# Expert weights loaded into the freed feed-forward blocks, and expert tiles placed in the slots of the loop's last five steps

## The reference

```python
x = x + attention0(layernorm(x))                    # 16 heads
x = x + feed_forward(layernorm(x))                  # silu(gate) * up, 256 -> 1024 -> 256
x = x + attention1(layernorm(x))                    # 16 query heads on 4 key heads
h = layernorm(x)
scores = einsum('btd,ed->bte', h, Wg)               # 8 experts
topk_s, topk_i = top_k(scores, 2)
w = einsum('btk,btke->bte', softmax(topk_s), onehot(topk_i))
for e in range(8):
    y = y + w[..., e:e+1] * ((silu(h @ W1[e].T) * (h @ W2[e].T)) @ W3[e].T)   # hidden 176
x = x + y
```

## Time and profile before

| | |
|---|---|
| three runs | 1286.82, 1291.46, 1289.36 us, median 1289.36 |
| the profiled execution | 1285.61 us, span 1283.9 us |
| busy | PE 86%, DVE 57%, ACT 44%, POOL 35% of the span |
| PE clock granted, mean | 0.91 of full speed |
| tiles | from 992.8 to 1244.4 us |
| gathers of group 1, adds, output | from 1244.4 us to the end |

### The profile page before, as it was taken

One profiled execution on the slowest core, in us unless ns is written; L12 is line 12 of the kernel. 1 busy time (PEld: TensorE's weight loads), 2 busy tenths in 40 slices (PEclk: granted clock), 3 DMA queues, 4 the chain that ended last, 5 costly groups with the idle time before them and its releaser, 6 DMA issues.

```text
span 1283.9 us, 27492 instructions
## 1 busy us (share of the span) xinstructions
PE 1105.1 (86%) x8482; PEld 908.3 (71%) x8482; DVE 737.3 (57%) x1985; ACT 569.1 (44%) x1252; POOL 447.6 (35%) x608
## 2 busy tenths in 40 slices
PE   3989999999989799999999999999774978997870
PEld 2766666667656698888888888888653857775750
DVE  3567676676753555566666666664547645444543
ACT  2145455554544344555555555553332534553330
POOL 4234444444432111224333343444355130014516
PEclk9599999999998999999999999998755978998885
DMA  6344444344440461001111111111222332334545
GB/s 217 110 119 139 117 135 116 118 140 117 132 115 27 140 210 34 22 25 42 42 40 40 40 44 40 40 42 62 79 94 70 104 116 79 99 108 139 153 130 166
DMA packets 98580, 122.17 MB, mean 95 GB/s; under 512 B 16054, under 2 KB 85884, under 8 KB 98492
## 3 DMA queue, kind: packets, MB, share of 16 engines
q1 hardware_dynamic: 91580, 102.17, 25.8%
q0 software_dynamic: 6912, 18.88, 4.6%
HBM read 64.37 MB, written 56.10 MB: 94 GB/s over the span
## 4 chain that ended last, share of the span: by engine, by line
PE 60%; DVE 14%; ACT 8%; issue 7%; POOL 4%; another core or an unknown queue 3%; DMA 1%; DVEq 1%; SPq 0%; POOLq 0%; ACTq 0%
PE bank L963 4%; PE bank L1579 3%; PE bank L876 3%; PE bank L1581 3%; PE bank L1580 3%; DVE a_negm L1291 3%; PE bank L878 2%; PE bank L877 2%; PE bank L583 2%; PE bank L600 2%; PE bank L608 2%; PE bank L598 2%; PE bank L623 2%; PE bank L599 2%
## 5 line engine op out<-in xcount | busy, mean ns | idle before, releaser
L1172 ACT ACTIVATE a_prob<-bank 128x512 f32<-128x512 f32 x192 | 114.2, 598 | 134.6 <-PE bank L963 134.1
L1579 PE MATMUL bank<-b_xF_hi,wff_hi 128*128 128x256 f32 x512 | 154.0, 301 | 2.2 <-DVE b_xF_lo L1939 1.4
L1291 DVE TENSOR_REDUCE a_negm<-bank 128x2 f32<-128x512 f32 (+1 forms) x192 | 129.7, 683 | 37.7 <-PE bank L930 37.7
L1580 PE MATMUL bank<-b_xF_lo,wff_hi 128*128 128x256 f32 x512 | 145.7, 285 | 0.1
L1581 PE MATMUL bank<-b_xF_hi,wff_lo 128*128 128x256 f32 x512 | 145.6, 284 | 0.0
L1396 POOL TENSOR_SCALAR_AFFINE_SELECT a_prob<-a_prob 128x1024 f32<-128x1024 f32 x64 | 70.0, 1094 | 169.2 <-ACT a_prob L1172 169.2
L820 POOL DMA_INDIRECT m_ring<-y_sorted,b_k_rows x64 | 61.7, 964 | 167.8 <-DMA y_sorted<-m_y 128.5
L930 PE MATMUL bank<-a_K,a_Q 48*128 48x256 f32 (+1 forms) x512 | 111.4, 319 | 0.0
L963 PE MATMUL bank<-a_Q,a_K 50*128 50x256 f32 (+1 forms) x512 | 106.8, 310 | 0.4 <-ACT a_prob L1172 0.4
L1947 DVE TENSOR_TENSOR b_hf<-bank,b_sg 128x256 f32<-128x256 f32 x128 | 53.9, 421 | 89.4 <-ACT b_sg L1802 85.4
L1579 PEld LDWEIGHTS bank<-b_xF_hi,wff_hi 128*128 128x128 f32 x512 | 97.9, 191 | 7.7 <-DVE b_xF_lo L1939 1.6
(11 more groups left out here) (269 smaller groups left out, 3214.7 us busy)
## 6 DMA issues: line engine op xcount, KB each, us to landing
scr<-a_split SPq DMA_DIRECT2D x64, 256.0 KB, 2.4
a_Q<-scr SPq DMA_DIRECT2D x192, 64.0 KB, 2.2
a_K<-scr SPq DMA_DIRECT2D x192, 64.0 KB, 2.3
m_xs<-x_sorted SPq DMA_DIRECT2D x78, 128.0 KB
y_sorted<-m_y SPq DMA_DIRECT2D x78, 128.0 KB
x_sorted<-b_r_zeros SPq DMA_DIRECT2D x1, 6016.0 KB, 19.9
parts<-b_split SPq DMA_DIRECT2D x16, 256.0 KB
out<-x_res SPq DMA_DIRECT2D x16, 256.0 KB
```

Of the source, the lines that this page charges most:

```text
L1172: nc.scalar.activation(o, src, ACT.Exp, scale=float(HD) ** -0.5).then_inc(S.exps, 1)
L1291: nc.vector.tensor_reduce(R.negm[:, p, j, c0:c0 + n], ps[bank][:, :].rearrange("p (h k) -> p h k", h=n), axis=AX.X, op=ALU.max, negate=Tru ...
L1579: pe.matmul(o, wh, xh, start=(c == 0), stop=False)
L1580: pe.matmul(o, wh, xl, start=False, stop=False)
```

## The change

1. **Weights.** The feed-forward's weights are laid out in eight blocks of 768 columns, block m holding all that slot m uses. Ten blocks of 768 make up the experts' weights. Their raw form is loaded straight into the place of `wff_lo` (`wraw` shares its memory), copied to `wff_hi` by ACT and replaced by the difference. Blocks 8 and 9, which the feed-forward never used, are loaded behind SP's step 14; blocks 0 to 5 in step 15, each once `down` of the last sequence has used it; 6 and 7 in step 16, between the store of sequence 14's queries and keys and the loads of their stacks. ACT's copies stand in (15,0), (15,1), (15,5), (15,6), (15,7) and (16,0) to (16,4); POOL makes the first six differences, all at the end of its step 15, DVE the last four in (16,1) to (16,4).
2. **Tiles in slots.** The loop ends with step 20 in place of 18. From (16,5) on each slot begins with one expert tile on PE, ACT and DVE, tiles 0 to 34; tile 35 and those behind it follow the loop. SP starts loading tiles behind step 16, and its step 17 comes behind the load of tile 9.
3. **Banks.** The tiles have one bank for transposes in and for `hT` together (0), one for the product (1) and one for `down` (2) while i < 21; from there the product alternates between 1 and 3, and `hT` has 5. So `up(k)` waits for the product of k-1 in the narrow part, `hT(k)` for the transposed tile k+2, and `xT(k)` for the subtraction of `hT(k-3)`.
4. **What `rest` did** for sequences 14 and 15 goes back into the steps 19 and 20.
5. **Tables.** `v_table` is cut into three parts: group 0's in (15,4), (15,6) and (18,4), group 1's in (20,4), (20,5) and (20,7).

```diff
-NMAIN = 12
+FF_BLOCK = 2 * NC * P + E
+NMAIN = WD_MAIN // FF_BLOCK
...
         wff_hi = sb("wff_hi", [P, WMAX], F32R)
+        with ExitStack() as raw_weights:
+            wraw = raw_weights.enter_context(nc.sbuf_tensor("wraw", [P, WMAX], F32))
         wff_lo = sb("wff_lo", [P, WMAX], F32R)
...
             def sp(eng):
                 for i in range(NTILES + 8):
+                    if i == 10:
+                        layer["sp_step"](eng, NSEQ + 1, 1)
...
+                        if i == 0:
+                            eng.wait_ge(layer["S"].up, NSEQ * INTER0 // P)
...
+            XT, DOWN = 0, 2
+
+            def up_bank(i):
+                return 1 if i < NARROW or i % 2 == 0 else 3
+
+            def hT_bank(i):
+                return XT if i < NARROW else 5
...
+                def xT(k):
+                    eng.wait_ge(S.loaded[k % 4], 16 * (k // 4 + 1))
+                    if k >= 1:
+                        eng.wait_ge(S.xT_lo, k)
+                    if k >= 3 and k - 3 < NARROW:
+                        eng.wait_ge(S.hT_lo, k - 2)
...
+                def up(k):
+                    eng.wait_ge(S.xT_lo, k + 1)
+                    if k >= 1:
+                        eng.wait_ge(S.h, k if k <= NARROW else k - 1)
...
+                def hT(k):
+                    eng.wait_ge(S.h, k + 1)
+                    if k < NARROW:
+                        eng.wait_ge(S.xT_lo, min(k + 3, NTILES))
+                    elif k >= 1:
+                        eng.wait_ge(S.hT_lo, k)
...
+                if i == 0:
+                    eng.wait_ge(layer["S"].h, NSEQ * INTER0 // P)
+                    eng.wait_ge(layer["S"].ffres, NSEQ)
+                    eng.wait_ge(S.table, 1)
+                    offsets(0)
+                    xT(0)
+                    xT(1)
+                    eng.wait_ge(wf.lo1, NMAIN)
+                    eng.wait_ge(wf.tail, 3 * NTAIL)
...
-            first, end, last = 6, 14, NSEQ + 2
+            def tile_of(t, m):
+
+                return NM * (t - NSEQ) + m - 5
+
+            def with_tile(t, m):
+                return isinstance(t, int) and t >= NSEQ and tile_of(t, m) >= 0
...
                     elif m > 2 and live(t):
                         pe_down(pe, t, m - 2)
+                    if with_tile(t, m):
+                        X1["pe"](pe, tile_of(t, m))
...
+            def main_block(k):
+
+                b = (k + NM) % NMAIN
+                return [w[:, b * FF_BLOCK:(b + 1) * FF_BLOCK] for w in (wff_hi, wff_lo, wraw)]
...
+            HI_AT = {(15, 0): 0, (15, 1): 1, (15, 5): 2, (15, 6): 3, (15, 7): 4, (16, 0): 5, (16, 1): 6, (16, 2): 7,
+                     (16, 3): 8, (16, 4): 9}
+            LO_AT = {(16, 1): 6, (16, 2): 7, (16, 3): 8, (16, 4): 9}
...
+            TABLE_AT = {(15, 4): (0, 0), (15, 6): (0, 1), (18, 4): (0, 2), (20, 4): (1, 0), (20, 5): (1, 1), (20, 7): (1, 2)}
...
-                if isinstance(t, int) and NSEQ <= t < NSEQ + 3:
-                    for n in range(4):
-                        p_weights(pool, 4 * (t - NSEQ) + n)
+                if isinstance(t, int) and t == NSEQ - 1:
+                    for k in range(NMAIN - len(LO_AT)):
+                        p_weights(pool, k)
...
                     sp_out(sp, t - 2, p)
+                    if isinstance(t, int) and t == NSEQ:
+                        sp_weights(sp, 8)
+                        sp_weights(sp, 9)
                     sp_stacks(sp, t - 2, p)
...
+            def sp_weights(sp, k):
+
+                b = (k + NM) % NMAIN
+                if b < NM:
+                    sp.wait_ge(S.down, NM * (NSEQ - 1) + b + 1)
+                if k >= 4:
+                    sp.wait_ge(wf.hi1, k - 3)
+                sp.dma_start(main_block(k)[2], w_moe[:, b * FF_BLOCK:(b + 1) * FF_BLOCK])\
+                    .then_inc(wf.in1[k % 4], 16)
+
+            first, end, last = 6, 14, NSEQ + 4
```

More of the change, by code:

```diff
@@ L482, in uses, with v_table @@
                 return len(range(k, n, depth))
-            def v_table(dve, n, g):
+            LINKED = (7, 12, 7)
+            CLEARED = sum(LINKED[:2]) + 2
+            COUNT = {(g, part): g * sum(LINKED) + sum(LINKED[:part]) + 2 * ((g, part) >= (0, 2)) for g in range(2) for part in range(3)}
+            NARROW = 21
+            def v_table(dve, g, part):
                 grp = TOKENS[g]
                 steps, tiles = grp.cap // P, grp.tiles
-                o = [S.count, n]
+                o = [S.count, COUNT[g, part]]
                 def linked(instruction):
@@ L495, in v_table @@
                 one = slice(0, P)
[L496 to L524, removed]
@@ L531, in v_table @@
-                nc.vector.tensor_copy(table[:, 1, :], R.local[0:1, 0:tiles]).then_inc(S.table, 1)
-                items = 4 * (grp.seqs[1] - grp.seqs[0])
-                mine = cols(4 * grp.seqs[0], items)
-                big = R.big[:, 0:items * NEXP].rearrange("p (i e) -> p i e", e=NEXP)
-                jump = R.load
-                linked(nc.vector.tensor_tensor(R.until, R.until, R.each, ALU.subtract))
-                linked(nc.vector.scalar_tensor_tensor(out=R.until, in0=R.until, scalar=-float(P), in1=R.base[:, g, :],
-                                                      op0=ALU.mult, op1=ALU.add))
@@ new lines, in dve @@
+                if i == 0:
+                    for k in range(2):
+                        nc.vector.memset(R.h[:, k, :], 0.0).then_inc(S.count, 1)
+                    xT(0)
+                    xT(1)
+                if i < NTILES:
+                    h(i)
+                if 1 <= i <= NTILES:
+                    hT(i - 1)
+                if i + 2 < NTILES:
+                    xT(i + 2)
+                if i == TOKENS[1].tile:
+                    eng.wait_ge(route.S.weights, NSEQ)
+                if i >= TOKENS[1].tile + 6:
+                    for _ in range(2):
+                        if done[0] < end_item[0]:
+                            add(eng)
@@ L804, in pool, with sums @@
+            def sums(eng):
+                while done[0] < len(items):
+                    add(eng)
             def pool(eng):
[L805 to L808 removed]
                 first = 0
@@ L2218, in run @@
                 for t in range(end, last + 1):
+                    if engine == "sp" and t == NSEQ + 1:
+                        return
                     step(eng, t, t % 2)
-            return dict(S=S, run=run, v_f_ln=v_f_ln, p_f_ln=p_f_ln, pe_oT=pe_oT, pe_out=pe_out, act_oT=act_oT, v_oT=v_oT, v_res=v_res)
+                if engine != "pool":
+                    for i in range(tile_of(last, NM - 1) + 1, NTILES + 2):
+                        X1[engine](eng, i)
+            return dict(S=S, run=run, v_f_ln=v_f_ln, p_f_ln=p_f_ln, sp_step=sp_step)
         def first_ln(eng, engine, old, new):
```

453 lines of the change are left out of this document (198 added, 255 removed).

## The result

Four runs of the changed kernel gave 1268.40 to 1281.25 us, median 1273.96, beside four of the kernel before with a median of 1288.94: ratio 0.9871, 95% interval 0.9837 to 0.9904, so 15 us or 1.3% faster. The forecast of 1280 had the sign; against its 9 us the gain was 1.6 times as large.

A forecast was written before the change was run, and what follows sets the result against it. Bound: the drain's chain of waits, then PE's work. 940.1 + 21.4 + 125.2 + 13.5 = 1100.2 against 1107.9 at tile 35, 7.7 us less; between 1277.9 and 1281.6 it chose 1280 us, 8-in-10 range 1248 to 1302.

The forecast's parts named there:

- part 1: Step 15 and start of step 16: POOL's differences delay the table (+9.7 us, bounds 0 to 12), DVE's add 1.1.
- part 2: Slots (16,5) to (16,7): waits, three tiles partly at half clock, a Silu table load and attention work, 21.4 us.
- step 17: Eight slots with a tile each: 22.4 us of tiles, 9.8 of attention work, 3.2 of stalls, 35.4 together.
- step 18: Eight slots with a tile each: 22.4 us of tiles, 7.3 of attention work, 5.2 of stalls, 34.9 together.
- step 19: Eight slots with a tile each: 21.5 us of tiles, 3.6 of attention work, 1.6 of stalls, 26.7 together.
- step 20, burst and scatters: Step 20's tiles, attention work and stalls, 28.2 us, plus POOL's twelve DMAs, 10.5, and scatters in steps 17 and 18, 3.
- (15,4) at nothing: Seven table operations in slot (15,4), where PE is full: 0 to 1.5 us, taken as 0.
- part 4: POOL's DMA bursts: twelve in a row in step 20, 10.5 us; scatters of fours in steps 17 and 18, 3.
- the marker: Start of tile 35's first matmul, first tile behind the loop: 1107.9 us before, 1100.2 forecast, nothing changing behind it.
- B: PE's pace holds: no POOL hold on DVE, stalls covered, narrow slots free; 30 us less, 1250; chance 0.20.
- C: Half clock among the tiles of steps 17 to 20: 4.32 us a slot, 1300 at one whole step; chance 0.24.
- D: Nothing moves: late blocks or loads leave tiles standing in (16,5) and step 17; 1288 us; chance 0.12.

The follow-up runs named there:

- e9: Changed kernel with group 0's first two table parts in slots (15,0) and (15,2) instead of (15,4) and (15,6); ratio to before 0.9897.
- e2: Changed kernel with POOL's six weight differences waiting until the second part of group 0's table is written; ratio to before 0.9876.
- e12: Changed kernel with POOL's six weight differences on DVE in (16,0) and (16,4), table parts in (15,0) and (15,2); 1270.81 us, ratio 0.9853.
- e1: Changed kernel with group 0's first two table parts in slots (14,4) and (14,6) instead of (15,4) and (15,6); ratio to before 0.9868.
- e6: Changed kernel without tiles in the slots: all tiles behind step 20, with two product banks; 1279.82 us, ratio to before 1.0174.
- e8: Changed kernel with POOL's eight fill DMAs of group 1 each waiting for a tile's product; 1241.09 us, ratio to before 0.986.

## Why the prediction was right, and where it was off

The forecast was right in sign and in where the time goes, and low in size: it set tile 35 at -7.7 us; it came at -16.5 on the chip of the result, and 3.4 were lost again behind it. The steps of the sum (from (16,1) to (16,5) before took 12.3, after 13.4):

| step of the sum | forecast | first chip | second chip |
|---|---|---|---|
| part 1: delay of (16,1) | 10.8 | 12.4 | 12.1 |
| and up to (16,5) | 0 | 1.0 | |
| part 2: start of the tiles to tile 3 | 21.4 | 17.6 | 18.6 |
| step 17 | 35.4 | 36.9 | 35.5 |
| step 18 | 34.9 | 34.1 | 35.3 |
| step 19 | 26.7 | 27.6 | 26.7 |
| step 20, burst and scatters | 41.7 | 32.7 | 23.4 |
| behind tile 35 | 0 | +3.4 | +0.4 |

- **Part 1.** Right in place and nearly in size: the table part lasted 9.9 us where 9.7 was said. The mechanism under it was half wrong. I let one operation be held for all four splits, after the 6.51 of the earlier trace rows; each was held for one. Why one was held for four in before stays open. The Trainium skill (SBUF — State Buffer, section "SBUF: two separate sides") has it so: an exclusive lock kept for one instruction. The rows of this kernel and of e9 agree with that. What was wrong is my price for it, about 6 us for the part: turn by turn it cost 9.9, since four operations were held for 0.9 to 1.6 each, 5.6 in sum, on top of the 4.3 that the part takes without splits (e2). That this met my 9.7, worked out from another picture, is luck. Splits five and six went on to hold two more (at 924.60 for 1.82 us and at 929.48 for 1.79; the upper bound of 12 that I named). What I had wrong is that the cost belongs to the table: e9 and e12 show that it belongs to the splits, and most of it, 6.9 us by e9's rows, stays when the table is moved away.
- **(15,4) at nothing:** right. From (15,1) to the projection in (15,6) the changed kernel takes 20.0 us and before 19.7, on the second chip. For the second part the slot matters: e1 showed no slack in (14,6).
- **Part 2** was 3 to 4 us too dear: the clock was 0.80 in it (0.75 on the second chip), and I had reckoned a part of the products at half clock for longer.
- **Steps 17 to 19** were within 1.6 us in sum, but two errors may lie under that. A narrow slot costs 0.79 more where it is bare, not 0.14: I took DVE's subtraction to delay the transposes once, by what it was late, and overlooked what stands behind them on PE, the reading of the offsets ahead of the transpose of h. In steps 17 and 18 attention work stands between the two and covers a part, and my stalls for ranking and exponentials made up the rest. The total was right; the division between them wasn't measured.
- **Step 20 and part 4** are the term that failed. The burst, 10.5, was sized well for this chip: tile 34 to 36 lost 12.6 us there and 3.0 on the other, so 9.6. But the scatters (3) did not show in steps 17 and 18; where one group did, in step 19 on the first chip, tiles 21 to 27 took 18.4 instead of 17.5. And the rest of step 20 took 23.4, not 28.2: tiles 27 to 34 came every 2.7 us, so its attention work (1.7) and its ranking (0.8) cost nothing, and of the 4.5 for the table's pieces 3.0 showed, in (20,7) and behind, 2.0 of it ahead of the marker. That is 9 us of the difference.
- **Behind the marker** 3.4 came back on this chip. 1.5 of it is tile 35 to 36 at half clock after the stall, the rest was not traced.
- **Rivals.** B (1250) asked for POOL not to hold DVE and for narrow slots at no price; both fail. C's half clock did not come: 0.91, 0.95 and 1.00 in steps 17 to 19. e6 shows what it is like when it does, without tiles to fill the slots. D is refuted by tile 35.

## What to carry to other kernels

Filling the slots of a draining pipeline with independent work gave 34 us at tile 35 (e6 against the changed kernel), and a higher clock for the drain's own work; bringing the inputs early is only what makes it possible, and gave nothing alone. Give a small job to the engine and the slot whose wait it can fill, and look up which instruction that wait stands in front of: one place further it is on the path (e1, e12). A POOL subtraction on SBUF beside a chain of small DVE operations with two inputs in SBUF cost the chain up to 1.6 of its 1.8 us for each; here it was cheaper to do the POOL work on DVE (0.93 against 1.8 us) than to move the chain.

## What the hardware showed that I had not expected

- The same kernel took 1274 to 1278 us on one kind of chip and 1246 on another. The difference went with waits of ACT whose end the trace can't name, 40 us in sum on the one and none on the other. All 19 of them in the kernel after begin within 1.6 us of the start of one of POOL's indirect DMAs. That these cause them was not tested where they occur: e8 ran on the second chip. At 1081.24 it was Silu, which waits for PE and DVE only, and both were through. What holds ACT stays open.
- A POOL subtraction held DVE operations with two inputs in SBUF (L345, L346, L519) and a multiplication by constants (L523, 1.70 us), and let a reduction (L521) and operations that read PSUM (L1984, L340) pass.
- Shared PSUM banks: 0.79 us on 2.66 a tile, 45 us at the end of the kernel when 54 tiles more share them (430.2 against 385.2).
